# Tokens of the line memory in the order 4p + j, and two-block maxima banks masked on TensorE and reduced by VectorE

## The chip, the cores and the metric

One NeuronCore of a Trainium2 chip runs the whole kernel. The metric is the device time of one execution in microseconds (us), as a median of several runs. The profile shows the engines TensorE (PE, with its weight loads as PEld), VectorE (DVE), ScalarE (ACT), GpSimd (POOL) and the DMA queues that SyncE (SP) and the others start.

## The reference

The input is 8 batches of 512 tokens of width 256. Per batch an attention block runs, then a layer norm, then a mixture of experts (4 experts, the best 2 of each token) with a second layer norm. What the change touches is in the attention block:

```python
scores = einsum('bhtd,bhsd->bhts', q, k) * scale; causal mask; softmax; seq_out = attn @ v      # 16 heads of 16
write_lines, read_lines = exterior(w1, w2), exterior(r1, r2)        # 6 numbers per token and head, unit length
outer = Jw[..., :, None] * Jw[..., None, :]                         # 6 x 6 per token and head
M_all[t] = decay**t * sum over s < t of outer[s] * decay**(-s)      # a decayed prefix sum over the tokens
rd_M = einsum('bhti,bhtij->bhtj', rd, M_all); score_M = rd_M . rd; score_M2 = rd_M . rd_M
gated = mean over heads of sigmoid(mem_score * mem_scale) * gate
x = layernorm(x + (seq_out + gated * mem_val) @ out_w.T + out_b)
```

## The kernel before

Each engine has its own program and runs it in order. All follow one list of stages written out by hand, `stages_of_a_step` (L56); `run` (L468) walks it and calls, on each engine, the engine's own part of the stage. `schedule` (L481) makes nine steps, 0 to 8. In step i the batch i is in its first half (maxima of scores, queries and keys of batch i+1), the batch i-1 in its middle (scores, values, lines, memory, late maxima) and the batch i-2 at its end (o_tokens, z, projection, layer norm, routing). So one step holds parts of three batches, and steps 2 to 6 hold all of them. After step 8 come the 35 tiles of the experts (L1518 and L1531 on TensorE), which the change leaves alone.

**Maxima.** For a numerically safe softmax every query row needs the maximum of its masked scores. `maxima` on TensorE (L1350) makes a piece of 512 columns in one of three PSUM banks: per pair of heads five pieces, `maxima_blocks` (L539), with the widths 512, 512, 384+128, 384+128 and 256+256. A batch has 40 pieces, 20 in `maxima` (batch i) and 20 in `late_maxima` (batch i-1). On VectorE `maxima` (L1918) takes one custom instruction for each block of a piece: it adds the mask `mask_ts`, takes the maximum, and a second small instruction reads the accumulator out into a column of `maxes`. TensorE writes piece n only when VectorE has read piece n-3 (`sm_read`), and `maxima_to_rows` (L1378) turns the 20 maxima of a half when all are read.

**Line memory.** The token of partition p and block c is 128c + p. The lines of a batch (`lines_in`, `lines_out`, the six products at L888, L891) are normalised by `norms` (L1930) on VectorE, and GpSimd makes `outer` (L909) and two more blocks in which a decayed earlier block is added (L915, L918). TensorE's `memory` (L1384) makes the prefix sums over tokens: for each head one matmul with a decay matrix of 128 x 128 over 144 columns (4 blocks of 36), and one with the matrix of the block before over 108 columns. It goes in six parts of three heads (the last of one) through the two banks `ms_ps`. VectorE's `memory` (L1954) multiplies each part by the read lines (432 numbers) and sums over six. In the next step `memory_scores` (L1968) makes the two scores from `rdm`, `memory_gates` and `gates` the gate.

**The order around it.** Late in a step VectorE's `rank` (L1894) makes the places of the routed rows; GpSimd's `scatter` (L837) then issues eight indirect DMAs and loads the next residual. SyncE's store (L606) writes the layer-norm output in blocks of 128 tokens. ScalarE's `exps` (L1103) takes the exponential of each scores piece; TensorE writes piece n when piece n-2 is done.

## Time and profile before

| | us |
|---|---|
| median of 3 runs | 1076.8 (1074.87 to 1082.2) |
| profiled execution | 1076.55 |
| its span | 1074.9 |
| TensorE busy | 948.6 (88%) |
| VectorE busy | 738.0 (69%) |
| ScalarE busy | 603.7 (56%) |
| GpSimd busy | 444.0 (41%) |

The 1.65 us between the profiled execution and its span lie outside the first and last instruction. A busy time of TensorE counts overlapping matmuls once, but each matmul's own time is far longer than the distance to the next one, so work on TensorE is read from starts. Steps 0 to 8 end at about 626 us, the experts at about 1026 us; the last 49 us are the final layer norm and the stores.

### The profile page before, as it was taken

The numbers are of one execution on the slowest core, as the hardware profiler recorded it, in microseconds if no ns is written. First come the engines' busy times: TensorE is split into PE (matmuls) and PEld (weight loads), VectorE is DVE, ScalarE is ACT, GpSimd is POOL, SyncE is SP. The second block draws the span as 40 slices with busy tenths as digits, with TensorE's granted clock in tenths as the row PEclk, the third lists the DMA queues.
The fourth block names the chain that finished last, engine by engine and source line by source line (L and its number), as shares of the span: only waits on it lengthen the run. The fifth ranks groups of instructions, "written<-read, shape, count | busy, mean of one in ns | idle before, by whom it ended". The sixth has DMA issues, their size and how long they took to land. (4 is left out here: it accounts for less than half of the span.)

```text
span 1074.9 us, 26814 instructions
## 1 busy us (share of the span) xinstructions
PE 948.6 (88%) x8038; PEld 686.6 (64%) x8039; DVE 738.0 (69%) x2668; ACT 603.7 (56%) x1358; POOL 444.0 (41%) x398
## 2 busy tenths in 40 slices
PE   3698999897998997989979889999989989999970
PEld 1244656554655564565545668888879869889860
DVE  4637797795896996978868668876555655555663
ACT  3155554562563554545535668776676656666653
POOL 6437064273363543654544633322322433222243
PEclk8689999998999999999999999999999989999995
DMA  4785103213124033032030453232333323323264
GB/s 140 247 216 141 31 22 124 56 57 117 38 71 119 24 95 85 2 125 55 21 129 12 139 188 85 45 51 48 49 46 60 73 49 53 48 49 49 41 204 159
DMA packets 60852, 90.38 MB, mean 84 GB/s; under 512 B 8700, under 2 KB 50192, under 8 KB 59696
## 3 DMA queue, kind: packets, MB, share of 16 engines
q1 hardware_dynamic: 45336, 62.20, 20.4%
q0 software_dynamic: 14112, 22.42, 11.2%
q10 hardware_dynamic: 1280, 4.19, 1.0%
q8 instruction: 67, 1.10, 0.5%
q14 instruction: 57, 0.47, 0.1%
HBM read 52.79 MB, written 35.86 MB: 82 GB/s over the span
## 5 line engine op out<-in xcount | busy, mean ns | idle before, releaser
L1926 DVE CUSTOM_DVE_ANT_0 junk<-sm,mask_ts 128x512 bf16<-128x512 f32 (+3 forms) x512 | 220.4, 487 | 58.0 <-PE sm L1366 55.8
L1110 ACT ACTIVATE arena_b<-st 128x512 f32<-128x512 f32 x320 | 180.9, 599 | 136.7 <-PE st L1328 89.8
L950 POOL DMA_INDIRECT sums<-arena_b x66 | 109.9, 1666 | 273.9 <-DVE arena_b L2135 263.6
L2098 DVE TENSOR_TENSOR arena_b<-arena_b 128x256 f16<-128x256 f32 x280 | 116.4, 427 | 109.6 <-ACT arena_b L1185 99.4
L1326 PE MATMUL st<-arena_a 128*128 128x384 f16 (+3 forms) x512 | 129.4, 309 | 29.0 <-issue 19.0
L1366 PE MATMUL sm<-arena_a 128*128 128x512 f16 (+3 forms) x512 | 113.7, 311 | 12.1 <-DVE maxes L1926 6.2
L1518 PE MATMUL st<-arena_b,arena_a 128*128 128x256 f16 x840 | 116.2, 276 | 1.6 <-ACT arena_b L1185 1.6
L1518 PE MATMUL sm<-arena_b,arena_a 128*128 128x256 f16 x840 | 115.1, 273 | 2.3 <-issue 2.3
L1531 PE MATMUL pv<-arena_a,arena_b 128*128 x864 | 116.7, 273 | 0.0
L1531 PE MATMUL sm<-arena_a,arena_b 128*128 x816 | 112.9, 274 | 3.1 <-issue 3.1
L1326 PEld LDWEIGHTS st<-arena_a 128*128 128x128 f16 x512 | 50.9, 99 | 87.0 <-issue 45.2
L1346 PE MATMUL pv<-arena_b 128*32 128x512 f32 (+3 forms) x1024 | 97.9, 478 | 8.1 <-ACT arena_b L1110 6.4
L1181 ACT ACTIVATE arena_b<-sm,arena_b 128x256 f32<-128x256 f32 x140 | 67.0, 478 | 67.5 <-PE sm L1518 48.1
L1181 ACT ACTIVATE arena_b<-st,arena_b 128x256 f32<-128x256 f32 x140 | 66.8, 477 | 60.0 <-PE st L1518 40.9
L844 POOL DMA_INDIRECT slots<-res,slot_i x64 | 62.8, 981 | 90.1 <-DVE slot_i L1915 72.7
L1328 PE MATMUL st<-mask_st,ident_b 128*128 128x128 bf16 x512 | 97.5, 224 | 0.0
L1518 PEld LDWEIGHTS sm<-arena_b,arena_a 128*128 x840 | 82.2, 98 | 13.6 <-issue 3.7
L1518 PEld LDWEIGHTS st<-arena_b,arena_a 128*128 x840 | 82.5, 99 | 13.1 <-issue 3.0
L1531 PEld LDWEIGHTS pv<-arena_a,arena_b 128*128 128x128 f16 x864 | 84.5, 98 | 9.9
L1531 PEld LDWEIGHTS sm<-arena_a,arena_b 128*128 128x128 f16 x816 | 79.9, 98 | 13.5 <-issue 4.0
L1366 PEld LDWEIGHTS sm<-arena_a 128*128 128x128 f16 x512 | 41.9, 100 | 57.5 <-DVE maxes L1926 29.1
L1284 PE MATMUL ms<-arena_b 128*128 128x208 f16 (+2 forms) x576 | 70.8, 275 | 4.3 <-DVE zs L2008 4.1
(335 smaller groups left out, 1756.5 us busy)
## 6 DMA issues: line engine op xcount, KB each, us to landing
arena_b<-slots SPq DMA_DIRECT2D x35, 260.0 KB
arena_a<-w SPq DMA_DIRECT2D x8, 1024.0 KB, 6.2
arena_b<-x_tr SPq DMA_DIRECT2D x8, 512.0 KB, 4.1
q_rows<-arena_b SPq DMA_DIRECT2D x32, 128.0 KB
k_rows<-arena_b SPq DMA_DIRECT2D x32, 128.0 KB
arena_a<-q_rows SPq DMA_DIRECT2D x32, 128.0 KB
arena_a<-k_rows SPq DMA_DIRECT2D x32, 128.0 KB
res<-x_tok POOLq DMA_DIRECT2D x8, 512.0 KB, 6.4
```

What stands on the lines that cost most here:

```text
L950: pool.indirect_dma_start(sums, bass.IndirectOffsetOnAxis(ap=token_now[:, 1 - par, m:m + 1], axis=0), y_out[1 - par][:, m, :], None, compu ...
L1110: act.activation(probs[:, q, :], st_ps[piece % 2][:, :], ACT.Exp, scale=SCORE_SCALE).then_inc(exp_done, 1)
L1181: act.activation(g_32[:, hc % 4, :], u_bank(hc)[:, 0:ROWS], ACT.Gelu, bias=b1_now[:, par, hc:hc + 1], scale=1.0 / W_SCALE).then_inc(gelu_d ...
L1284: last = pe.matmul(out, xs[b_par][:, kc, shift:shift + P], ws[:, kc, cols:cols + n_cols], start=start and kc == 0 and n == 0, stop=kc == K ...
L1326: pe.matmul(out[:, at:at + width], ks[:, h % 2, h // 2, s * P:(s + 1) * P], qs[:, h // 2, s * P:T], start=m == 0, stop=False, skip_group_c ...
L1328: last = pe.matmul(out[:, at:at + P], ident_b[:, :], mask_st[:, :], start=False, stop=True, skip_group_check=True)
L1346: last = pe.matmul(out[32 * hl:32 * hl + 32, s * P:T], v_aug[:, s, 4 * g + hl, :], probs[:, slot, col:col + width], start=cls == 0, stop=c ...
L1366: last = pe.matmul(sm_ps[n % 3][:, at:at + width], qs[:, j, tile * P:(tile + 1) * P], ks[:, p, j, 0:width], start=m == 0, stop=True, skip_ ...
L1518: last = pe.matmul(u_bank(hc)[:, 0:ROWS], w_by_expert[:, up_expert, at:at + P], xs[par][:, kc, :], start=kc == 0 and n == 0, stop=kc == KC ...
L1531: last = pe.matmul(y_ps[1 - par][:, m * D:(m + 1) * D], gs[1 - par][:, hc, m * P:(m + 1) * P], w_by_expert[:, down_expert, at + lo * CHUNK ...
L1926: last = dve.tensor_tensor_reduce(junk[:, n % 3, at:at + width], sm_ps[n % 3][:, at:at + width], mask_ts[:, T - width:T], 1.0, NEG, ALU.ad ...
L2098: dve.tensor_tensor(g_lo[par][:, hc, :], g_32[:, hc % 4, :], g_hi[par][:, hc, :], ALU.subtract).then_inc(hid_done, 1)
```

## The change

Five things change together.

1. **Order of tokens.** Partition p now holds the tokens 4p, 4p+1, 4p+2, 4p+3. Matmuls that used 128 neighbouring columns as weights now use every fourth one (`n::C`): `lines_in`, the half of `values_in` that makes `mem_val`, and the transposes of `o_tokens`. Input, store and token numbers follow.
2. **Prefix sums.** GpSimd adds the four outer products of a partition (three additions instead of two multiplications and two additions), and TensorE needs one matmul of 36 columns for each head, in two parts of eight heads. What a token gets from the up to three earlier tokens of its own partition (six pairs) is computed on GpSimd as vectors, partly before it waits for the norms (`pair_gain`), partly after `outer_done` (`near_rows`, `near_done`), and added by VectorE in `memory_scores`.
3. **Maxima.** For the pieces with two blocks TensorE adds the mask by a matmul of 256 columns (24 per batch), and VectorE takes the whole bank with one plain maximum. The last piece of a half is followed by a small reduction and a copy.
4. **Tables.** Powers of the decays are half as many and one small table is made by GpSimd.
5. **The list of stages** is written anew in places; `rank` stands ahead of maxima 17, and the second part of `memory` behind values 8.

```diff
-        ("maxima", 17), ("rank", 0), ("first_expert", 0), ("maxima", 18), ("scores", 33), ("memory", 2), ("maxima", 19), ("values", 8),
-        ("scores", 34), ("scores", 35), ("memory", 3), ("memory", 4), ("scores", 36), ("scores", 37), ("maxima_rows", 0), ("memory", 5),
-        ("first_rows", 0), ("scores", 38), ("values", 9), ("scores", 39), ("values", 10), ("values", 11),
+        ("scores", 31), ("maxima", 16), ("tables", 0), ("scores", 32), ("values", 7), ("rank", 0), ("first_weights", 3),
+        ("first_expert", 0), ("maxima", 17), ("maxima", 18), ("scores", 33), ("maxima", 19), ("values", 8), ("memory", 1),
+        ("scores", 34), ("maxima_rows", 0), ("scores", 35), ("scores", 36), ("scores", 37), ("first_rows", 0), ("scores", 38),
+        ("values", 9), ("scores", 39), ("values", 10), ("values", 11),
...
+                    for own in range(C - 1):
+                        m, at = C - 1 - own, FIRST_PAIR[own]
+                        seen = chain(pool.tensor_tensor(pair_parts[:, at:at + m], read[:, own + 1:C, :, ::-1],
+                                                        write[:, own:own + 1].broadcast_to([P, m, H, NL]), ALU.mult))
...
                     pool.wait_ge(ninv_done, n_of(b + 1))
...
+                    for to, of in ((0, 1), (2, 3), (0, 2)):
+                        if (to, of) != (2, 3):
+                            pool.wait_ge(pool_chain, n_of(seen))
+                        last = pool.tensor_tensor(outer[:, to, :, :], outer[:, to, :, :], outer[:, of, :, :], ALU.add)
...
+                    last.then_inc(outer_done, 1)
...
+                    pool.tensor_tensor(near_rows[:, 3:C], near_rows[:, 3:C], pair_parts[:, 5:6], ALU.add).then_inc(near_done, 1)
...
                     if n == 0 and later(i, 2):
-                        act.wait_ge(sq_done, n_of(b))
+                        act.wait_ge(near_done, n_of(b))
...
-                    project(out[:, :], 1 - par, COL_VM, 512, 2 + n * P, True).then_inc(vm_ready, 1)
+                    project(out[:, 0:D], 1 - par, COL_VM, D, slice(2 + n * P, 2 + n * P + P), True)
+                    project(out[:, D:2 * D], 1 - par, COL_VM + D, D, slice(2 + n, 2 + T, C), False).then_inc(vm_ready, 1)
...
+                    if piece % 5 >= 2:
+                        blocks = sm_ps[n % 3][:, :].rearrange("p (n t) -> p n t", t=P)
+                        last = pe.matmul(blocks[:, 2:4] if piece % 5 < 4 else blocks[:, 1::2], mask_st[:, :], ident_b[:, :].unsqueeze(1).broadcast_to([P, 2, P]),
+                                         start=False, stop=True, skip_group_check=True)
...
+                        last = pe.matmul(out[:, hl * size:(hl + 1) * size], decay_t[:, heads * q + hl, :], outer[:, 0, heads * q + hl, :],
+                                         start=hl == 0, stop=hl == heads - 1, skip_group_check=True)
...
-                        last = pe.transpose(out[:, g * P:(g + 1) * P], o_t[:, g, n * P:(n + 1) * P], ident[:, :])
+                        last = pe.transpose(out[:, g * P:(g + 1) * P], o_t[:, g, n::C], ident[:, :])
...
+                    if kind < 2:
+                        col = 32 * kind + 4 * j + 3
+                        dve.tensor_tensor_reduce(junk[:, n % 3, :], bank[:, :], mask_ts[:, :], 1.0, NEG, ALU.add, ALU.max, maxes[:, col:col + 1]).then_inc(sm_read, 1)
+                    elif kind < 4:
+                        dve.tensor_reduce(of_blocks[:, kind - 2, at, :], bank[:, :].rearrange("p (n t) -> p n t", t=P), AX.X, ALU.max).then_inc(sm_read, 1)
...
+                            dve.tensor_reduce(of_half[:, :, :, 2], of_blocks[:, :, :, 0:3], AX.X, ALU.max)
+                            last = dve.tensor_copy(of_half[:, :, :, 0], of_blocks[:, :, :, 3])
...
+                    for n in range(C):
+                        rows = read_scaled[:, H * n + heads * q:H * n + heads * q + heads, ::-1]
+                        last = dve.tensor_tensor(mr[:, n], ms_ps[q][:, 0:heads * NL * NL].rearrange("p (h a e) -> p h a e", a=NL, e=NL),
+                                                 rows.unsqueeze(2).broadcast_to([P, heads, NL, NL]), ALU.mult)
...
+                    m_chain(dve.tensor_reduce(rdm[:, q].rearrange("p c h a -> p (c h a)"), mr.rearrange("p c h a e -> p (c h a) e"), AX.X, ALU.add))
...
+                    s_chain(dve.tensor_tensor(by_half(rdm[:, :, 1:C]), by_half(rdm[:, :, 1:C]), near_rows[:, 1:C].rearrange("p c (q h) e -> p q c (h e)", q=2), ALU.add))
```

## Rows read from the trace of the kernel before

**Rows 1.** Busy time by stretch: us, busy us (instructions) per engine, clock, DMA, GB/s
```profile
core 0: us, PE busy (x) PEld busy (x) DVE busy (x) ACT busy (x) POOL busy (x), PEclk, DMA share, GB/s
343.00:414.70 71.70, 65.88 (x554) 41.00 (x553) 57.62 (x220) 37.62 (x84) 36.06 (x31) 0.98 0.28 77
...
626.00:1026.00 400.00, 389.53 (x3500) 345.72 (x3499) 250.53 (x841) 273.25 (x627) 121.06 (x77) 0.99 0.32 57
```

**Rows 2.** The same view, step 5 cut into stretches
```profile
343.00:359.00 16.00, 15.78 (x139) 9.97 (x139) 14.85 (x48) 9.64 (x26) 5.77 (x3) 1.00 0.38 83
359.00:375.00 16.00, 14.76 (x109) 9.01 (x108) 14.04 (x59) 9.26 (x21) 10.95 (x11) 1.00 0.12 34
375.00:391.00 16.00, 15.88 (x136) 9.12 (x135) 14.91 (x62) 11.13 (x24) 10.71 (x9) 1.00 0.22 67
391.00:408.00 17.00, 14.10 (x137) 11.20 (x133) 13.02 (x52) 4.59 (x10) 5.84 (x6) 1.00 0.37 118
```

**Rows 3.** Timeline of TensorE: start us, us, instruction [idle before it and its releaser]
```profile
374.91 0.39 PE L1381 MATMUL sm<-ident,maxes 128*16 128x128 f32 x2 [0.71 <-DVE maxes L1926]
...
392.05 0.41 PE L1396 MATMUL ms<-outer,arena_a 128*128 128x144 f32 x2
...
392.51 0.43 PE L1396 MATMUL ms<-outer,arena_a 128*128 128x144 f32 x2
```

**Rows 4.** Timeline of VectorE, one round of five maxima pieces in step 0
```profile
44.63 0.69 DVE L1926 CUSTOM_DVE_ANT_0 junk<-sm,mask_ts 128x512 bf16<-128x512 f32 x1
...
45.24 0.69 DVE L1926 CUSTOM_DVE_ANT_0 junk<-sm,mask_ts 128x512 bf16<-128x512 f32 x1
...
47.92 0.69 DVE L1926 CUSTOM_DVE_ANT_0 junk<-sm,mask_ts 128x512 bf16<-128x512 f32 x1
```

**Rows 5.** Timeline of VectorE, a memory part and the instruction behind it, step 5
```profile
395.14 0.61 DVE L1961 TENSOR_TENSOR mr<-ms,lines 128x432 f32<-128x432 f32 x1 [0.25 <-PE ms L1398]
395.78 0.60 DVE L1964 TENSOR_REDUCE rdm<-mr 128x72 f32<-128x432 f32 x1
396.30 0.68 DVE L1926 CUSTOM_DVE_ANT_0 junk<-sm,mask_ts 128x512 bf16<-128x512 f32 x1
```

**Rows 6.** Groups of instructions by line and shape, VectorE: busy us, mean ns, idle before
```profile
L1964 DVE TENSOR_REDUCE rdm<-mr 128x72 f32<-128x432 f32 x40 | 24.1, 603 | 1.4
...
L1979 DVE TENSOR_TENSOR mr<-rdm,lines 128x384 f32<-128x384 f32 x8 | 4.9, 612 | 0.0
...
L1983 DVE TENSOR_TENSOR mr<-rdm 128x384 f32<-128x384 f32 x8 | 7.5, 932 | 0.3
```

**Rows 7.** Chain that ended last, in the experts, and 16 narrow matmuls on TensorE
```profile
792.54 0.66 PE st L1518 x6
...
316.98 1.90 PE L1441 MATMUL ms<-w_r,z_t 128*128 128x4 f32 x16
```

**Rows 8.** Groups of weight loads on TensorE, by shape
```profile
L1284 PEld LDWEIGHTS ms<-arena_b 128*128 128x128 f16 x576 | 39.8, 98 | 26.5 <-DVE zs L2008 6.5 <-issue 0.4
...
L1408 PEld LDWEIGHTS ms<-ident,o_t 128*128 128x128 f32 x128 | 14.9, 148 | 6.3 <-DVE zs L2008 3.9 <-issue 1.2 <-ACT o_t L1122 0.2
```

**Rows 9.** GpSimd in step 5 (timeline), and its narrowest line products by shape
```profile
378.27 0.86 POOL L900 TENSOR_TENSOR t<-lines,ninv 128x384 f32<-128x384 f32 x1 [4.55 <-DVE ninv L1942]
...
388.04 1.40 POOL L918 TENSOR_TENSOR outer<-outer 128x576 f32<-128x576 f32 x1
...
L888 POOL TENSOR_TENSOR t<-pts 128x128 f32<-128x128 f32 x16 | 10.4, 672 | 0.0
```

**Rows 10.** Timeline of all engines around the scatter of step 5
```profile
400.63 1.01 POOL L844 DMA_INDIRECT slots<-res,slot_i  x1 [11.18 <-DVE slot_i L1915]
...
407.86 0.60 ACT L1110 ACTIVATE arena_b<-st 128x512 f32<-128x512 f32 x1 [6.06 <-remote]
...
408.51 0.28 PE L1326 MATMUL st<-arena_a 128*128 128x256 f16 x1 [3.41 <-issue]
...
412.32 0.31 DVE L1961 TENSOR_TENSOR mr<-ms,lines 128x144 f32<-128x144 f32 x1 [4.56 <-remote]
```

More of the change, by code:

```diff
@@ L76, in stages_of_a_step @@
-        ("x1_rows", 3), ("first_weights", 2), ("scores", 27), ("maxima", 11), ("maxima", 12), ("maxima", 13), ("scores", 28),
-        ("gates", 0), ("logits", 0), ("values", 6), ("scores", 29), ("scores", 30), ("maxima", 14), ("memory", 0), ("memory", 1),
-        ("first_weights", 3), ("maxima", 15), ("scores", 31), ("maxima", 16), ("tables", 0), ("scores", 32), ("values", 7),
-        ("maxima", 17), ("rank", 0), ("first_expert", 0), ("maxima", 18), ("scores", 33), ("memory", 2), ("maxima", 19), ("values", 8),
@@ L798, in powers_of_decays @@
                 pool.wait_ge(decay_set, 2)
-                n, done, zero = 1, 0, 2 * P - 1
+                n, done, zero, power = 1, 0, P - 1, 5
                 while n < T - 1:
@@ new lines, in step @@
+                    last.then_inc(outer_done, 1)
+                    seen = chain(pool.tensor_tensor(write_unit.rearrange("p c h e -> p (c h) e"), lines[:, 0, 0:3 * H, :],
+                                                    ninv[:, 0, 0:3 * H].unsqueeze(2).broadcast_to([P, 3 * H, NL]), ALU.mult))
+                    pool.wait_ge(pool_chain, n_of(seen))
+                    for own in range(C - 1):
+                        m, at = C - 1 - own, FIRST_PAIR[own]
+                        to = near_rows[:, 1:C] if own == 0 else pair_parts[:, at:at + m]
+                        seen = chain(pool.tensor_tensor(to, pair_gain[:, at:at + m].unsqueeze(3).broadcast_to([P, m, H, NL]),
+                                                        write_unit[:, own:own + 1].broadcast_to([P, m, H, NL]), ALU.mult))
@@ L1391, in memory @@
                             pe.wait_ge(turned, 4)
-                    out = bank(q % 2, cs_read, 6 * b + q + 1)
-                    size = C * NL * NL
-                    for hl, h in enumerate(range(3 * q, min(3 * q + 3, H))):
-                        pe.matmul(out[:, hl * size:(hl + 1) * size], decay_t[:, h, 0:P], outer[:, h, 0:C, :].rearrange("p c e -> p (c e)"),
-                                  start=hl == 0, stop=False, skip_group_check=True)
-                        last = pe.matmul(out[:, hl * size:(hl + 1) * size - NL * NL], decay_t[:, h, P:2 * P],
-                                         outer[:, h, C - 1:C + 2, :].rearrange("p c e -> p (c e)"), start=False, stop=True, skip_group_check=True)
+                    out = bank(q, cs_read, 2 * b + q + 1)
+                    size, heads = NL * NL, H // 2
+                    for hl in range(heads):
+                        last = pe.matmul(out[:, hl * size:(hl + 1) * size], decay_t[:, heads * q + hl, :], outer[:, 0, heads * q + hl, :],
+                                         start=hl == 0, stop=hl == heads - 1, skip_group_check=True)
                     last.then_inc(cs_ready, 1)
@@ L2231, in lay_out @@
     return {
[L2232 removed]
+        "x_tok": x.reshape(B, P, C, D), "x_tr": x.reshape(B, T, KC, P).transpose(3, 0, 2, 1),
         "w_proj": by_part(w.T), "qk_bias": qkv_b[order].reshape(4, P).T,
```

246 lines of the change are left out of this document (145 added, 101 removed).

## Prediction

> **What bounds the kernel now.** I read the page first, then the busy time by stretch, then the timeline of one full step, then the groups by shape, last the waits. The experts take 400 us with TensorE nearly always busy [rows 1], and the change does not touch them; what it can move lies in the first 626 us, steps 0 to 8. Steps 2 to 6 last 71 to 77 us each, and I take step 5, 343.0 to 414.7 us, as their pattern: 71.7 us, TensorE busy 65.9, VectorE 57.6, GpSimd 36.1 [rows 1]. A share for the whole step misleads, so I cut it [rows 2]. From 343 to 375 (call it the early part: late maxima, o_tokens, lines, values, projection) VectorE is busy 28.9 of 32 us and TensorE idles at places, for VectorE's maxima among them (0.71 us before the maxima rows) [rows 3]. From 375 to 391 both are busy over 90%. From 391 VectorE is dense until about 404; then an odd end follows, read in the last part of the sum. So VectorE bounds the early part, both engines together bound the middle, and a saving of one alone is not paid out whole.
>
> **What each part costs.** First the maxima on VectorE. A round of five pieces takes 47.92 - 44.63 = 3.29 us from start to start where VectorE is never idle, a piece of 512 columns 0.61 [rows 4]. Afterwards two pieces stay as they are (2 x 0.61). The three others become one plain reduction of 512 numbers each. No row shows a reduction out of PSUM. The nearest is the one of 432 numbers in SBUF: 603 ns, and 396.30 - 395.78 = 0.52 us to the next start [rows 5, 6]. 80 numbers more at the pace between 384 and 512 would add under 0.1, so I take 0.60 us; as bounds I keep 0.52 (the row itself) and 0.69 (the custom instruction's own time [rows 4]). The round is then 2 x 0.61 + 3 x 0.60 = 3.02, 0.27 less; four rounds in a half save 1.1 us. The small reduction, its wait and the copy at the end of a half I take at 0.45 together (bounds 0 and 0.6, the latter one whole reduction of 432 numbers [rows 6]). Net -0.6 us per half, -1.2 per batch. As many numbers pass through VectorE as before (512 for 384 + 128): only the per-instruction part is saved.
>
> The memory on VectorE: a part of 432 costs 0.64 + 0.52 = 1.16 us [rows 5], five of them and a small one about 6.4 us a batch. After it there are per half four products of 288 and one sum of 1152. At the same pace (0.64 for 432, about 1.05 ns a number above a fixed 0.15) four products are about 1.6 and the sum 1.3, so 5.75 for both halves: -0.65 us. The same 2304 numbers pass again.
>
> Memory scores: one addition of 288 more and the product of 384 cut in two. Rows: 612 ns for a product of 384 with two inputs in SBUF, but 932 ns for the next one of the same size [rows 6]. I take +0.8 us (0.5 to 1.3). VectorE per batch: -1.2 - 0.65 + 0.8 = -1.05 us.
>
> TensorE. A head costs 392.51 - 392.05 = 0.46 us in memory [rows 3], 16 heads 7.4 us. Afterwards a head is two passes of 36 columns behind a full fp32 weight load. The nearest row is 16 passes of 4 columns with fp32 weights in 1.90 us, 0.12 each [rows 7]: 32 x 0.12 = 3.8. That saves 3.6 us a batch, all of it in the middle of the step. The masks add 24 matmuls of 256 columns, 0.66 / 6 = 0.11 us each [rows 7]: +2.6, 1.3 early and 1.3 in the middle. The weights taken with a step of four columns (lines, half of values, o_tokens) are not in the trace. Below, they cost nothing more. Above, I double the load of each: 98 ns for fp16 and 148 for fp32 [rows 8]. A pass that is shorter than its load then waits for it: for 48 matmuls of lines and 16 transposes that is up to 3.6 us a batch, all early. I take 0.9. TensorE per batch: -3.6 + 2.6 + 0.9 = -0.1, split into +2.2 early and -2.3 in the middle.
>
> A rule speaks against this. Row: contiguous fp32 weights of a transpose load in 148 ns, fp16 ones in 98 [rows 8]. The Trainium skill, page "SBUF — State Buffer", section "Door 1: The DMA port swizzle", says in a note that SBUF lines are 16 bytes and that accesses reach full rate only with two or more hits in a line. A step of four fp16 numbers would have two hits, one of four fp32 numbers one, so by it only the o_tokens would pay, at most 1.8 us of early TensorE time a batch instead of my 0.9; no row here shows a stepped load.
>
> GpSimd gets seven new instructions before it waits for the norms, in a wait of 4.55 us in step 5 [rows 9]. The two wide products are priced like others of their size. The narrow ones step through memory, like those of 128 numbers at 672 ns [rows 9]. Together about 3.9 us, so the wait covers them; with no cover they would delay `outer_done` by their own length, and a slack stands behind it: GpSimd is done at 388.04 + 1.40 = 389.4 [rows 9] and TensorE starts memory at 392.05 [rows 3], 2.6 us later. After the norms: one more product of 384 (0.86 [rows 9]), two multiplications of outer less, one addition more: equal within 0.3 us. About 3 us of near rows follow `outer_done`; the 11.18 us in which the scatter waits for VectorE's slots [rows 10] cover them, and so behind them in GpSimd's queue the eight scatters and the residual's load are not later. `near_done`, at about 392.5, holds ScalarE's lines_out and VectorE's memory scores of the next step, which begins at 414.7 [rows 1], 22 us later. Were it late, the exponentials would stand behind it on ScalarE and the late maxima on VectorE. The new tables on GpSimd stand in an idle stretch before step 1. Half as many powers, shorter turns and a larger SyncE store block are hidden as well: zero, 1 us at most.
>
> **The sum.** Step 0 has one half of maxima with VectorE as the bound: -0.6. Middle of a full step: VectorE gives -0.6 - 0.65 = -1.25 and TensorE -2.3; both are dense, so between them, nearer to the lesser: -1.6. Early part: VectorE +0.2, TensorE +2.2, part of which fills its idle places: +0.3. That is -1.3 a step. Eight steps (1 to 8; the last has no first half of maxima, but is TensorE's and ScalarE's, where -3.6 counts more) give -10.4. Total -11.0. Against the profiled execution: 1076.55 - 11.0 = 1065.55, and I say 1065.5. That execution lies 0.25 below the median of the runs, so the same holds there.
>
> The end of a step is what I can price least. While GpSimd issues the eight scatters (from 400.63 on), a ScalarE exponential starts 6.06 us late, TensorE idles 3.41 us, and the last memory product on VectorE comes 4.56 us late, though its inputs were there [rows 10]. The new list puts `rank`, and so the scatter, ahead of maxima 17 to 19 and memory 1. I count no change: behind rank VectorE needs 3 x 0.61 + 0.45 = 2.3 us for the three maxima, and its late start begins at 412.32 - 4.56 = 407.8, 7 us after the first scatter (ScalarE's at 401.8, 1.2 us after it).
>
> **Rivals.**
> *A. The whole of TensorE's saving is paid, and the end of the step shrinks.* TensorE is dense in the middle [rows 2]; if VectorE's waits for it hide inside its busy share, -2.3 a step counts, and an earlier scatter takes 1 us off the end of steps 2 to 7: 8 x -2.3 - 6 - 0.6 = -25, 1051.5. Against it: VectorE is dense in the same place.
> *B. The saving is swallowed early.* Masks and stepped weights put 2.2 us on TensorE where it has few idle places; if they cost 1 us more a step than I say, -11 + 8 = -3 is left: 1073.5.
> *C. Stepped weights load at half speed.* Early TensorE +4.9 instead of +2.2, of which idle places (1.5 us of 32 by the busy rows [rows 2], and what hides between) take nearly all of the first half: 8 x (+2.5) - 11 = +9, 1085.5. For it speaks the page above in part; against it that a load usually hides behind the matmul ahead of it.
> *D. The scatter meets the maxima.* If the late start of 4.56 us [rows 10] falls on maxima 17 to 19, TensorE stands at the maxima rows, which precede scores 35, and cannot pass: 6 steps x 4.5 - 11 = +16, 1092.5, slower. It decides when VectorE still has a maximum of the first half to take when its late starts begin, somewhere between 1.2 and 7 us after the first scatter.
>
> **How the numbers follow.** About 1% can be told from no change here, 10.8 us. Chances: the forecast 0.40 (1061 to 1070 is its own range), A 0.20, B 0.22, C 0.08, D 0.10. The forecast straddles the 1% line at 1066.0: of its 0.40 I count 0.23 as faster. With A that is 0.43. Same is 0.17 + 0.22 + most of C (0.05) = 0.44; slower is D and the rest of C, 0.13. The range leaves out the far end of A and of D: 1050 to 1084.
>
> **What would show it.** The reduction from PSUM at about 690 ns, next start after 0.60. Memory on TensorE at 3.8 us a batch. Stepped weight loads no longer than 98 and 148 ns, or else C. GpSimd's wait for the norms shrunk from 4.55 us to under 1, with no wait of TensorE for outer. Steps 2 to 6 about 1.3 us shorter each, and the experts at 400 us. I am wrong if a new wait stands before the maxima rows (D), or if a step changes by over 3 us without the middle having changed.

## The result, and the profile after

The kernel after takes 1094.8 us (1091.3 to 1100.3, 6 runs) where the kernel before takes 1080.0 on the same chip: a ratio of 1.0146, interval 1.0109 to 1.0182. It is slower, and outside the range. The later runs were on other chips, so each is compared with the kernel before on its own chip. On chip 11 (before 1078.8) the ratio of the same kernel was 1.0145 [1.0100, 1.0190]; on chip 9 (before 1054.1) it was 1.0015 [0.9993, 1.0037], no difference. (The first chip's number is not recorded.) So there are two things to explain: why 11 us of gain came out nowhere, and what costs 1.5% on chips like the first and nothing on chips like chip 9.

I cut every trace at the same three marks: the transfer to `o_t` of the last values, which ends a step; the late maxima rows on TensorE; and again the end. "Early" is from a step's end to the late maxima rows of the next step, "middle" from there to that step's end. Below are the early part of step 2 and both parts of step 5 (on chip 9 only the middle of step 5), first in the kernel before on the first chip (its step 5 whole is in [rows 1]). The expectations below call the early part of step 2, the first that is cut so, "the early part of step 1".

```profile
core 0: us, PE busy (x) PEld busy (x) DVE busy (x) ACT busy (x) POOL busy (x), PEclk, DMA share, GB/s
120.06:152.10 32.04, 30.72 (x245) 18.92 (x243) 28.32 (x106) 19.03 (x46) 13.26 (x11) 1.00 0.15 40
342.80:374.91 32.11, 30.66 (x244) 18.89 (x243) 28.80 (x106) 19.01 (x46) 16.72 (x13) 1.00 0.25 59
374.91:414.22 39.31, 35.16 (x310) 22.11 (x310) 28.63 (x114) 18.33 (x39) 19.34 (x18) 0.96 0.29 92
```

The kernel after, same chip:

```profile
113.87:146.88 33.01, 32.20 (x280) 23.31 (x279) 27.84 (x74) 18.95 (x46) 14.50 (x14) 1.00 0.14 39
340.60:377.88 37.28, 34.67 (x280) 24.71 (x279) 29.75 (x74) 19.27 (x46) 16.91 (x15) 0.92 0.19 46
377.88:418.06 40.18, 33.49 (x290) 19.21 (x291) 28.28 (x78) 18.81 (x38) 24.47 (x29) 0.91 0.29 92
```

The kernel before on chip 9:

```profile
119.21:151.24 32.03, 30.72 (x245) 18.91 (x243) 28.28 (x106) 18.97 (x46) 13.26 (x11) 1.00 0.13 40
363.71:397.15 33.44, 33.33 (x310) 21.81 (x310) 28.61 (x114) 18.15 (x38) 16.62 (x16) 1.00 0.31 95
```

The kernel after on chip 9:

```profile
117.73:150.73 33.00, 32.20 (x280) 23.32 (x279) 27.83 (x74) 18.95 (x46) 14.49 (x14) 1.00 0.14 39
364.85:398.00 33.15, 31.59 (x290) 18.90 (x291) 28.25 (x78) 18.65 (x39) 20.94 (x26) 1.00 0.29 92
```

Read the rows at full clock (PEclk 1.00) first. The early part of step 2 grew from 32.04 to 33.01 us on the first chip and from 32.03 to 33.00 on chip 9; it is 33.02 on chip 11. The middle on chip 9 went from 33.44 to 33.15: TensorE is busy 1.74 us less and the time is 0.29 less. VectorE's busy time fell by only 0.36. On the first chip the middle of step 5 is 6 to 7 us longer in either kernel, and that is not the change's doing.

Summed over the seven early parts (steps 2 to 8) and the middles of steps 1 to 7, from the profiled executions (us; "experts" is all that follows step 8, the final layer norm and stores too):

| | to late rows of step 1 | early | middle | step 8 | experts | span |
|---|---|---|---|---|---|---|
| before, first chip | 89.2 | 232.6 | 266.6 | 37.3 | 449.2 | 1074.9 |
| after, first chip | 84.2 | 250.9 | 264.0 | 37.4 | 456.2 | 1092.6 |
| before, chip 9 | 88.3 | 247.8 | 231.1 | 32.8 | 449.8 | 1049.8 |
| after, chip 9 | 85.9 | 247.9 | 233.4 | 33.1 | 456.4 | 1056.8 |
| after, chip 11 | 82.3 | 245.6 | 265.9 | 37.7 | 455.2 | 1086.7 |

The first column scatters between 80.7 and 89.2 over the runs of all kernels, so I read nothing from it. The loss on the first chip is 18.3 us early and 7.0 in the experts; the middles give 2.6 back and the first column 5.0. On chip 9 the profiled execution after is 7.0 us longer, and 6.6 of it lie in the experts.

The operations themselves, in the kernel after on chip 9, grouped by shape (count, busy us, mean ns, idle before them and its cause):

```profile
L1988 DVE TENSOR_REDUCE maxes_of_blocks<-sm 128x4 f32<-128x512 f32 x128 | 84.1, 685 | 25.8 <-PE sm L1420 25.5
L2032 DVE TENSOR_TENSOR outer_home<-ms,t 128x288 f32<-128x288 f32 x64 | 24.8, 450 | 4.8 <-PE ms L1452 4.8
L2036 DVE TENSOR_REDUCE rdm<-outer_home 128x192 f32<-128x1152 f32 x16 | 21.6, 1353 | 0.6
```

They are as forecast (about 690 ns the reduction, 1.3 us the sum). The prices of what VectorE was given were right; what happened to its other instructions was not foreseen.

In step 7 of the kernel after a new wait stands ahead of the maxima rows (first number the start, in brackets the idle time before it):

```profile
528.63 0.59 PE L1437 MATMUL sm<-ident,maxes 128*16 128x128 f32 x2 [2.74 <-DVE maxes L1997]
```

It is the same 2.74 us on the first chip and on chip 11. In this step alone `first_expert` gives VectorE 2.6 us of small instructions for the experts' order and tables (523.9 to 526.5), and the new list has it ahead of maxima 17 to 19 and the maxima rows ahead of scores 35 to 37. The middle of step 7 on chip 9 went from 33.28 to 35.92 us, at a clock of 1.00 and 0.90, while those of steps 2 to 6 became 0.2 to 0.3 shorter.

**GpSimd's "hidden" work stretches VectorE's.** Rows of the timeline of step 5 in the kernel after on chip 9 (start, length). VectorE's small instructions:

```profile
365.37 0.48 DVE L1902 TENSOR_TENSOR rs<-rs 128x4 f32<-128x4 f32 x1
366.97 0.43 DVE L2008 TENSOR_SCALAR n<-n 128x128 f32<-128x128 f32 x1
369.64 0.78 DVE L1910 SCALAR_TENSOR_TENSOR shift<-mean_var,rs 128x4 f32<-128x4 f32 x1
381.94 0.56 DVE L1931 TENSOR_TENSOR beaten<-lg 128x4 f32<-128x4 f32 x1
```

and GpSimd's at the same times:

```profile
365.16 0.67 POOL L918 TENSOR_TENSOR pts<-pts 128x288 f32<-128x288 f32 x1
366.89 0.43 POOL L923 TENSOR_TENSOR pts<-pts,pair_table 128x96 f32<-128x96 f32 x1
369.55 0.86 POOL L929 TENSOR_TENSOR t<-lines,own_power 128x384 f32<-128x384 f32 x1
381.83 0.64 POOL L958 TENSOR_TENSOR t<-t,pts 128x192 f32<-128x192 f32 x1
```

Add start and length: VectorE's end at 365.85, 367.40, 370.42 and 382.50, GpSimd's at 365.83, 367.32, 370.41 and 382.47. An instruction of VectorE on four numbers ends when GpSimd's wide one does. In the kernel before GpSimd stood in a wait of 4.55 us when the first two of these came, as in [rows 9], and between two instructions when the third did; they took (VectorE in step 5 on chip 9):

```profile
364.24 0.15 DVE L1844 TENSOR_TENSOR rs<-rs 128x4 f32<-128x4 f32 x1
365.51 0.23 DVE L1938 TENSOR_SCALAR n<-n 128x128 f32<-128x128 f32 x1
367.98 0.16 DVE L1852 SCALAR_TENSOR_TENSOR shift<-mean_var,rs 128x4 f32<-128x4 f32 x1
```

Over all eight batches on chip 9 the means went from 334 to 724 ns (`shift`), 151 to 362 (`rs`), 227 to 362 (the norms' maximum), and together from 632 to 1001 ns for the three comparisons of the logits: 1.1 us a batch. The Trainium skill, page "SBUF — State Buffer", section "Who interferes with whom", says that a VectorE instruction with two inputs in SBUF contends with a GpSimd instruction that reads SBUF, and that the later one waits for the whole of the other. The ends of `rs`, `shift` and `beaten`, 0.01 to 0.03 us after GpSimd's, agree; the norms' maximum (0.08 us after) has one input, so this sentence does not cover it. No run took GpSimd's new work away, so that this is what makes VectorE late in the middle is argued from these rows, not shown by an edit.

The kernel before has such meetings too, and on chip 9 they are larger than the change. VectorE's four gated sums into `zs` take 1.67 us together when alone; in step 8 of before_again (VectorE, GpSimd's residual and bias additions, TensorE):

```profile
545.44 5.87 DVE L2018 SCALAR_TENSOR_TENSOR zs<-arena_a,gated,zs 128x256 f32<-128x256 f32 x4
545.65 2.50 POOL L872 TENSOR_TENSOR res<-res,out_b 128x1024 f32<-128x1024 f32 x1 [8.59 <-DMA res<-x_tok]
548.12 2.52 POOL L875 TENSOR_TENSOR mv_odd<-mv_odd,mem_b 128x1024 f32<-128x1024 f32 x1
...
552.06 0.34 PE L1366 MATMUL sm<-arena_a 128*128 128x384 f16 x1 [2.90 <-DVE maxes L1926]
```

Single `zs` sums of 2.6 us instead of 0.48 stand there in steps 3, 5, 6, 7 and 8 of the kernel before and in steps 3, 5, 6 and 7 of the kernel after; on the first chip and chip 11 in none. So on chip 9 it matters where the additions fall: the early parts of steps 2, 3 and 4 grew by 1.0, 1.3 and 1.5 us, those of steps 7 and 8 shrank by 2.0 each, and the sum is equal. In it TensorE is busy 216.2 us before and 225.7 after; its idle time fell from 31.6 to 22.3.

**What the first chip adds.** Two things can be seen after the end of step 4: the residual's addition on GpSimd meets VectorE's near rows, and TensorE's lines then wait for VectorE's `zs` and run on at a lower clock. The timeline of the kernel after on the first chip, GpSimd's row, VectorE's and TensorE's:

```profile
344.81 2.36 POOL L887 TENSOR_TENSOR res<-res,out_b 128x1024 f32<-128x1024 f32 x1 [4.60 <-DMA res<-x_tok]
...
345.14 2.35 DVE L2054 TENSOR_TENSOR rdm<-rdm,t 128x288 f32<-128x288 f32 x1
...
351.99 4.57 PE L1333 MATMUL ms<-arena_b 128*128 128x64 f16 x36 [1.95 <-DVE zs L2088]
```

and the busy times of the stretch of the lines, of its part at half clock, and of the end of step 5, same kernel:

```profile
351.99:356.56 4.57, 4.57 (x38) 3.75 (x39) 4.13 (x11) 1.76 (x6) 0.00 (x0) 0.63 0.00 0
353.10:356.50 3.40, 3.40 (x24) 2.65 (x22) 2.96 (x10) 0.98 (x4) 0.00 (x0) 0.50 0.00 0
411.10:421.40 10.30, 7.17 (x42) 3.61 (x43) 2.24 (x7) 2.99 (x5) 3.46 (x4) 0.50 0.49 134
```

The addition of 288 numbers takes 2.35 us there and 2.38 in the next step; in the other steps, and on chip 9, where the two do not meet, it takes 449 ns. But the wait is not shown to come from the meeting: TensorE waits 2.25, 2.22 and 2.08 us for `zs` in steps 3, 7 and 8, where they do not meet. The granted clock was 1.00 before TensorE's wait and 0.63 over the lines that followed it: 3.4 us of that stretch at 1.2 GHz. In the kernel before the lines of step 5 had no such wait and ran at 1.00. Over the seven early parts the granted clock was 1.00, 0.96, 0.91, 1.00, 1.00, 1.00, 1.00 before and 1.00, 0.95, 0.88, 0.92, 0.95, 0.94, 0.95 after. If TensorE was busy throughout, the missing share of the clock times the length of each part is 4.8 us before and 15.0 after. These 10.2 us and 7 x 1.0 at full clock are 17.2 of the 18.3.

Most of the lost clock begins before the early part, in a step's last microseconds. Of the 29.5 us at 1.2 GHz in the seven early parts after, 22.7 are the ends of stretches that began in the step before, as at 411.10 above (the step ends at 418.06), where TensorE waits 1.38 and 2.44 us for ScalarE's exponentials, two of which start 2.3 us late; only 6.8 us, in steps 5 and 8, follow a wait for `zs`. In the kernel before such stretches reach 10.0 us into the early parts.

### The profile page after: what moved, and what is told of

The parts are those of the page before. It is cut to its first block and busy times, and to the rows that moved or that the text cites. A ratio compares the mean times of both kernels' runs of the same rounds, so it can differ in the third digit from the quotient of the medians.

```text
span 1092.6 us, 26611 instructions
## 1 busy us (share of the span) xinstructions
PE 950.1 (87%) x8170; PEld 702.9 (64%) x8171; DVE 735.4 (67%) x2127; ACT 604.5 (55%) x1357; POOL 507.2 (46%) x512
## 5 line engine op out<-in xcount | busy, mean ns | idle before, releaser
L1001 POOL DMA_INDIRECT sums<-arena_b x66 | 117.8, 1785 | 271.7 <-DVE arena_b L2215 261.3
L1986 DVE CUSTOM_DVE_ANT_0 junk<-sm,mask_ts 128x512 bf16<-128x512 f32 x128 | 84.9, 684 | 67.3 <-PE sm L1416 66.8
L1416 PE MATMUL sm<-arena_a 128*128 128x512 f16 (+3 forms) x512 | 116.3, 307 | 14.1 <-DVE maxes L1986 6.9
L1396 PE MATMUL pv<-arena_b 128*32 128x512 f32 (+3 forms) x1024 | 94.5, 467 | 18.3 <-ACT arena_b L1159 11.3
L1988 DVE TENSOR_REDUCE maxes_of_blocks<-sm 128x4 f32<-128x512 f32 x128 | 84.2, 685 | 25.7 <-PE sm L1420 25.5
L1585 PEld LDWEIGHTS sm<-arena_a,arena_b 128*128 128x128 f16 x816 | 80.5, 99 | 13.6 <-issue 3.6
L1333 PE MATMUL ms<-arena_b 128*128 128x256 f16 (+2 forms) x768 | 75.6, 256 | 10.6 <-DVE zs L2088 10.5
```

What stands on the lines that cost most here:

```text
L1001: pool.indirect_dma_start(sums, bass.IndirectOffsetOnAxis(ap=token_now[:, 1 - par, m:m + 1], axis=0), y_out[1 - par][:, m, :], None, compu ...
L1396: last = pe.matmul(out[32 * hl:32 * hl + 32, s * P:T], v_aug[:, s, 4 * g + hl, :], probs[:, slot, col:col + width], start=cls == 0, stop=c ...
L1416: last = pe.matmul(sm_ps[n % 3][:, at:at + width], qs[:, j, tile * P:(tile + 1) * P], ks[:, p, j, 0:width], start=m == 0, stop=True, skip_ ...
L1585: last = pe.matmul(y_ps[1 - par][:, m * D:(m + 1) * D], gs[1 - par][:, hc, m * P:(m + 1) * P], w_by_expert[:, down_expert, at + lo * CHUNK ...
L1986: dve.tensor_tensor_reduce(junk[:, n % 3, :], bank[:, :], mask_ts[:, :], 1.0, NEG, ALU.add, ALU.max, maxes[:, col:col + 1]).then_inc(sm_re ...
L1988: dve.tensor_reduce(of_blocks[:, kind - 2, at, :], bank[:, :].rearrange("p (n t) -> p n t", t=P), AX.X, ALU.max).then_inc(sm_read, 1)
```

## Experiments

Ratios are to the kernel before, run beside each kernel on its chip. Chip 1 (masks_only, no_masks, memory_behind_rank, contiguous_weights), 9 and 12 are like one another, with middles of 32 to 35 us in most full steps; chip 11 is like the first. The kernel after itself was not run on chips 1 and 12; the stretches of runs there are set against those of chip 9. (splits_off_the_adds, on chip 12, leaves these stretches as they are and has the same 33.00 and 33.15 us.)

**One part alone.** masks_only is the kernel before with the lines of the diff that touch `maxima`, on TensorE and VectorE; no_masks takes them out of the kernel after.

> The kernel before with one part of the change: the masks of the small maxima blocks on TensorE and plain reductions on VectorE; token order and order of the stages as before. Theory 1 (TensorE has no idle place in the early part of a step, 1.5 us of 32, so each matmul added there is paid): 12 masks of 0.11 us early = +1.3 us in each of steps 1 to 8, +10 in all, and about -0.3 a step in the middle from VectorE: about +8 us, 1088. Theory 2 (VectorE bounds the early part, as the prediction had it): -0.6 us a half, -8 to -9 in all: 1071.

> The kernel after without the masks on TensorE: maxima as in the kernel before, token order, memory and order of the stages as in the kernel after. Theory 1 (masks are paid on TensorE): about 8 us shorter than the kernel after, 1087. Theory 2 (VectorE bounds): 8 us longer than the kernel after, 1103. If the token order alone makes the loss, this is 1090 or more.

Masks alone 1.0039 [1.0012, 1.0067], the rest alone 1.0011 [0.9977, 1.0046]. By stretches at full clock: masks alone make the early part of step 2 32.33 (+0.3, not +1.3) and the middle 34.35 (+0.9); the token order, memory and list alone 32.78 (+0.75) and 33.45 to 33.60 (0 to +0.15). So the 3.6 us that TensorE saves in memory gave nothing by themselves, masks by themselves cost, and together the middle comes out at -0.3: TensorE's saving pays for TensorE's masks and little else. Both theories fell for the early part: the masks are neither paid in full there nor a gain. The token order and the work that comes with it carry three quarters of the early loss.

**Weights with a step of four.**

```diff
-                        last = pe.transpose(out[:, g * P:(g + 1) * P], o_t[:, g, n::C], ident[:, :])
+                        last = pe.transpose(out[:, g * P:(g + 1) * P], o_t[:, g, n * P:(n + 1) * P], ident[:, :])
```

and the slices `2 + n::C`, `1 + n::C` of `values_in` and `lines_in` likewise.

> The kernel after with contiguous weights in o_tokens, lines and the tokens' half of values, in place of those taken with a step of four columns; so tokens of another order are taken there and the output is wrong, with the same number of operations of the same shapes. Theory 1 (weight loads on a dense TensorE are paid): the 96 passes of lines and values fall from 9.8 to about 8.5 us a step and the 16 transposes from 2.5 to 2.1: -1.7 us a step, -14 in all, 1081. Theory 2 (the waits for zs on VectorE decide): at most -4, 1091.

0.9984 [0.9959, 1.0010]; the early part of step 2 is 32.92 instead of 33.00, the middle 33.16 as before. The o_tokens' loads themselves, by shape, stepped in the kernel after on chip 9:

```profile
L1462 PEld LDWEIGHTS ms<-ident,o_t 128*128 128x128 f32 x128 | 18.0, 210 | 7.1 <-DVE zs L2088 4.3 <-issue 1.1 <-ACT o_t L1171 0.7
```

and contiguous in this experiment:

```profile
L1462 PEld LDWEIGHTS ms<-ident,o_t 128*128 128x128 f32 x128 | 15.1, 151 | 7.0 <-DVE zs L2088 4.1 <-issue 1.4 <-ACT o_t L1171 0.7
```

210 against 151 ns, and 112 against 100 in the mean for the fp16 ones: the step costs the load, but hardly the time (0.1 us a step). My upper bound for the fp32 ones was twice their load; the trace shows 1.4 times.

**Which queue the middle hangs on.** one_product_of_four takes 2.3 us a step from VectorE, memory_twice gives 3.5 to TensorE:

```diff
-                    for n in range(C):
+                    for n in range(1 if later(i, 2) else C):
                         rows = read_scaled[:, H * n + heads * q:H * n + heads * q + heads, ::-1]
```

```diff
-                    for hl in range(heads):
+                    for hl in [*range(heads), *range(heads)]:
```

> The kernel after, which from step 2 on leaves out three of the four products in each half of memory (2 x 3 x 0.39 us of VectorE's queue, all in the middle of the step); the memory's result is wrong, TensorE's, ScalarE's and GpSimd's work is the same. Theory 1 (what TensorE saved in the middle has become waits for VectorE's queue, which is as long): the middle, 33.15 us from the late maxima rows to the step's end, becomes 1.5 to 2.3 us shorter, and the end of step 8 comes 10 us or more earlier. Rival (ScalarE's exponentials and the last values set the middle): under 0.5 us a step.

> The kernel after with TensorE's memory passes made twice (the second round overwrites the first): 32 more passes, 3.5 us a step, all in the middle; nothing else changes. Theory 1 (what TensorE saved there has become slack, 1.6 us of 33.15 by the busy rows and up to 3 in waits): the middle grows by 0.5 to 2 us, not by 3.5. Rival (TensorE still bounds the middle, and the saving was lost elsewhere): it grows by 3 to 3.5, end of step 8 25 us later.

one_product_of_four: 0.9935 [0.9895, 0.9975]; the middle is 32.38 instead of 33.15, so 0.8 of the 2.3 us are paid. memory_twice, on chip 11: 1.0322 [1.0270, 1.0374]; the middles of steps 2 to 5 are 41.6 to 43.2 instead of 39.9 to 40.0, +2.1 in the mean of the four, and step 8 is 3.6 longer. The only one of the four at full clock, step 2, gives +1.5; the others ran at 0.88, 0.88 and 0.96. The whole time rose by 23.2 us over after_third for 28 us of added passes. So on chip 11, with the lower clock, what is added to TensorE is paid for the larger part, and on chips 9 and 12 what is taken from either engine for the smaller: neither theory is the whole. I read it as two queues of one length, of which the shorter only waits for the other.

**The order of the stages.**

> The kernel after with one stage moved: the first half of memory (4 products and a sum, 2.9 us on VectorE) stands behind rank instead of three maxima pieces ahead of it. Theory A (the end of a step is pinned to its first scatter: 13.6 us behind it in steps 2 to 5 of both kernels): the scatter comes 2 to 2.9 us earlier and the end of steps 2 to 8 with it, 14 to 20 us in all, 1075 to 1081. Theory B (the last exponentials and values on TensorE and ScalarE set the end): within 3 us of the kernel after. Theory C (late starts on VectorE now meet the last maxima of the half, rival D of the prediction): a new wait ahead of the maxima rows and a longer step, 1100 or more.

> The kernel after with the first half of memory behind rank, as in memory_behind_rank. On a chip with late starts during the scatters (before at 1075 us or more): theory A (the end of a step is pinned to its first scatter) gives the scatter 2.1 us earlier and the step's end 1.5 to 2.1 us earlier in steps 2 to 8, 10 to 15 us below the kernel after there, ratio 1.000 to 1.005; rival (late starts now meet VectorE's last maxima or memory): 1.0145 or more. On a chip without them: 0.998 as in memory_behind_rank.

> The kernel before with its memory 0 and 1 (2.3 us on VectorE) behind rank. With late starts: theory A gives the scatter 1.5 to 2.3 us earlier and 10 to 15 us less, ratio 0.987 to 0.99; rival: no change or more, since the late starts meet more of VectorE's work. Without them TensorE is dense in the middle (33.3 of 33.4 us), and theory A gives no change, 0.998 to 1.002.

All three edits move only entries of the list: ("memory", 0), in the last ("memory", 0) and ("memory", 1), to just behind ("rank", 0). Results: 0.9979 [0.9951, 1.0008] on chip 1; 1.0118 [1.0091, 1.0144] and 1.0036 [1.0016, 1.0057] on chip 11. The first of the eight scatters of step 5 on chip 11, in the timeline of the kernel after:

```profile
403.15 1.01 POOL L859 DMA_INDIRECT slots<-res,slot_i  x1 [8.42 <-DVE slot_i L1973]
```

and with memory behind rank:

```profile
401.47 1.01 POOL L838 DMA_INDIRECT slots<-res,slot_i  x1 [6.29 <-DVE slot_i L1952]
```

Counted from the late maxima rows that is 26.5 and 24.4 us: the scatter did move by 2.1. The end did not follow: it lay 13.4 us behind the first scatter in steps 2 to 5 and now lies 16.9 to 17.7 behind, and the middle grew from 40.0 to 41.5 to 42.1. In the kernel before, that of step 5 grew from 39.3 (first chip) to 42.8. My theory A, suggested by an end at 13.5 to 14.1 us behind the scatter in steps 3 to 5 of both kernels, was a coincidence.

What the middle lost, the early part won back: with memory behind rank on chip 11 all seven early parts of the kernel after run at a clock of 1.00, 231.1 us in sum instead of 245.6, against middles of 279.1 instead of 265.9. The half-clock stretches now end before the step does. With the same place of memory in both kernels the early parts of steps 2, 3, 5 and 6 are 33.0 against 31.8 to 32.0 us: the added 1.0 us of a step, on this chip too. The two ratios, 1.0118 and 1.0036, lie 0.8% apart, where after_third alone is at 1.45%. On chip 11 and the first chip, what VectorE and ScalarE still have to do when the scatters start is what starts late. The list of waits calls the cause "remote": no instruction of this core is seen to release it (us in total, times, longest). In the kernel before on the first chip:

```profile
ACT arena_b L1110 <- remote: 43.7, 12, 8.2
DVE mr L1961 <- remote: 21.3, 5, 5.2
```

In the kernel after there:

```profile
ACT arena_b L1159 <- remote: 18.5, 6, 3.7
```

In the kernel before with memory behind rank, on chip 11:

```profile
DVE mr L1940 <- remote: 40.5, 6, 7.5
ACT arena_b L1089 <- remote: 33.5, 14, 5.2
```

More of VectorE's memory behind the scatters, more of it late: 40.5 us instead of 21.3. The lists of waits of chips 1, 9 and 12 have no such wait among their longest, and on chip 9 the end of step 5 lies 7.7 us (before) and 6.6 us (after) behind the first scatter. On chip 1 the edit makes the middle 0.9 longer too, and its 0.9979 is no gain that can be told.

> The kernel after with the first half of memory behind rank (as in memory_behind_rank) and the memory scores behind the last of the four o_tokens. Theory 1 (TensorE's wait of 2.0 to 2.4 us for zs, behind VectorE's memory scores, is paid in every step): 2 us less in each of steps 1 to 8 than memory_behind_rank, 14 to 16 us, ratio to before 0.983. Rival (VectorE is as late for the following maxima, and the wait moves there): no change, ratio 0.998.

> scores_behind_tokens without the masks on TensorE. Theory 1 (a matmul added to TensorE in the early part is paid, 1.3 us a step, and VectorE's 0.6 there not): 5 to 8 us less than scores_behind_tokens. Rival (with the waits gone VectorE bounds): 3 to 8 us more.

1.0012 [0.9978, 1.0045] and 1.0027 [1.0004, 1.0050]: taking the masks out as well makes no difference that can be told, so neither theory of reordered_no_masks came true. The waits of TensorE from the middle of step 1 to the end of step 8, in memory_behind_rank:

```profile
PE ms L1312 <- DVE zs L2067: 6.8, 4, 2.1
```

and in scores_behind_tokens:

```profile
PE ms L1312 <- ACT pts L1128: 6.6, 4, 2.0
```

The same lines wait as often and as long, now for ScalarE's `pts`: the rival was right, the wait moved, if to another engine than it said.

> The kernel after with the stages in the order of the kernel before (memory 0 and 1 in the places of its memory 1 and 3). Theory 1 (the loss is in the work, the order only moves waits): ratio to before 0.998 to 1.004, early part of step 1 33.0 or 0.2 less. Rival (the new order makes the loss, o_tokens 1 ahead of scores 1, z 0 early, rank ahead of maxima 17 to 19): early part of step 1 32.3, middle 32 or less, ratio 0.99.

On chip 11, 1.0089 [1.0054, 1.0124] with middles of 39.0 instead of 39.9 and the early part of step 2 at 33.05. The new order carries up to 0.6 of the 1.5%, in the middle; the early loss is the work's. The intervals of this and of after_third touch, so its size is not certain.

**The early part and the near rows.**

> The kernel after without the addition of the near rows on VectorE (0.45 us alone, 2.35 where it met GpSimd's residual addition), so the memory's result lacks them. Theory 1 (VectorE's memory scores stand ahead of the zs that TensorE waits for, 2.0 to 2.4 us in some steps): the early part of step 1, 33.0 us, becomes 32.5, and the other steps 0.5 to 1 less. Rival (TensorE's added passes make the early part): 33.0 stays.

> The kernel after with the masks on TensorE only for the first half of the heads, whose maxima lie in the middle of a step; the late maxima as in the kernel before. Theory 1 (in the early part TensorE is dense and pays 12 x 0.11 us, VectorE's 0.6 is not paid back): 1.0 to 1.3 us less from a step's end to the late maxima rows where the clock is full (33.0 before the edit in step 1), end of step 8 6 to 10 us earlier. Rival (VectorE bounds there): 0.6 us more a step.

near_add_left_out drops the first addition of `memory_scores`; masks_in_the_middle has `if piece % 5 >= 2 and not half_no` on TensorE and the old pieces on VectorE for the second half. On chip 11 the first gives 1.0082 [1.0058, 1.0107], and 32.76 early in step 2; the second, on chip 12, 1.0030 [0.9988, 1.0072] and 32.77. Each is worth 0.2 of the 1.0, the steps of the weights 0.1. About 0.4 of the early us stays without an owner. Against after_third the ratio fell from 1.0145 to 1.0082, more than 0.2 us a step would give, but the intervals touch. TensorE still waits 1.2 to 1.8 us for `zs` in five steps without the addition, so it is not what makes these waits.

**The experts.** The change touches none of their work, and still they took 7 us more in both pairs, all of it before tile 8 (from VectorE's first instruction of tile 0 to that of tile 8: 89.9 and 102.9 us on the first chip, 94.1 and 103.4 on chip 9; tile 0 starts before step 8 ends, so this stretch can grow by more than the 7 us). Some sums' adds were issued by GpSimd in 5.4 us, usually 1.55. splits_off_the_adds moves VectorE's weight splits from the first to the second half of tiles 1 to 5; splits_and_masks has both edits.

> The kernel after with the experts' weight splits (1024 numbers, two inputs in SBUF, 1.2 us each on VectorE) taken from the first half of tiles 1 to 5 into the second half, so that none follows the start of a scattered sum add. Theory 1 (an add's issue on GpSimd of 5.4 or 3.9 us, usual 1.55 to 1.75, is held up by VectorE's splits that run at the same time): no issue over 2.8 us is left, and the stretch from tile 0 to tile 8, 101 us in after_again, comes down to 90 to 94. Rival (the sums' traffic or the order of the tokens makes them long): they stay, and the stretch is 99 or more.

> Both edits of splits_off_the_adds and masks_in_the_middle together. Theory 1 of both: the two gains add, 14 to 18 us below the kernel after, ratio to before 0.985 to 0.99. Rival of either: that one's gain is missing.

GpSimd's sums in the kernel after on chip 9, and below them TensorE's wait for the slots in tiles 0 to 8:

```profile
L1001 POOL DMA_INDIRECT sums<-arena_b x66 | 117.7, 1783 | 266.3 <-DVE arena_b L2215 256.0 <-issue 10.4
...
PE ms L1311 <- DMA arena_b<-slots: 5.4, 3, 3.4
```

The same two with the splits moved, and a wait that is new:

```profile
L1001 POOL DMA_INDIRECT sums<-arena_b x66 | 107.8, 1633 | 275.0 <-DVE arena_b L2215 264.7 <-issue 10.4
...
PE ms L1311 <- DMA arena_b<-slots: 2.8, 3, 1.2
PE st L1572 <- DVE arena_a L1689: 4.4, 1, 4.4
```

The long issues are gone (the longest left is 2.4 us) and the waits for slots halved, so theory 1 is right on the adds; but TensorE now waits 4.4 us for one of the moved splits (L1689), and the stretch from tile 0 to tile 8 is 101.6 us instead of 103.4 (99.2 instead of 101.1 from tile 1 to 9, which is what the expectation counts), not 90 to 94. The ratios are 1.0021 [0.9978, 1.0064] and 1.0076 [1.0044, 1.0107]. Over all runs the stretch lies between 88.8 and 103.4. The new order of the tokens alone does not make it long: the four runs that have it together with memory 0 behind rank are at 88.8 to 94.7, with a step 8 that is 1.5 to 6 us longer. What makes it 94 in one kernel and 103 in another stays open, and so does why splits_and_masks has the highest ratio on chip 12.

**The same kernels again.**

> The kernel before, unchanged, for its trace on the chip of this call (on the chip of the first experiments the end of a step lay 6.6 to 8 us behind its first scatter, on the first chip 13.6). Ratio 1.00. If the chip makes the difference, its end of step lies 7 to 8 us behind the first scatter; if the edits made it, 13.6.

> The kernel after, unchanged, on the same chip. If the loss is TensorE's added work in the early part and the waits there (a cause that every chip has), the ratio is 1.01 or more again, with 3 to 5 us more from a step's end to the late maxima rows and 1.5 us less from there to the maxima rows. If the loss came from the late starts during the scatters, the ratio is 1.00 or less where these are absent.

> The kernel after, unchanged, on the chip of this call. If 1.0146 was that chip's and that pair of executions' own, the ratio is 0.998 to 1.004 again and the middle of a step 33.15 us; if the change costs this everywhere, 1.01 or more and the middle 40 us as on the first chip.

0.9996 [0.9959, 1.0033], 1.0015 [0.9993, 1.0037] and 1.0145 [1.0100, 1.0190], read above. The chip makes the late starts: end behind first scatter 7.7 us in before_again, 13.6 in the kernel before on the first chip. On chip 9 the early parts are equal in sum, 247.8 and 247.9 us, though TensorE has 1.0 us more to do in each: it fills idle time that the `zs` sums which meet GpSimd, shown above, leave in either kernel. That is read from the rows and not shown by an edit. (The early part of step 4 is long in either for another reason, a wait for the rows of the next batch: 4.2 us for `q_rows` before, 3.6 for `k_rows` after.) That a ratio near 1.0145 comes with the late starts is seen on the first chip and chip 11; what in them makes the change dearer beyond the clock was not tried. No kernel that computes all of the reference beat the kernel before by more than its interval.

## Why the prediction was wrong, point by point

- **The operations.** Reduction from PSUM, memory's products and sum and its passes on TensorE (3.85 us for 3.8): right within 5%. The stepped fp32 loads lie between my two bounds. (The 3.6 and 1.8 us for them cannot be worked out from [rows 8], where 48 x 98 + 16 x 148 ns are 7.1 us; at 0.1 us measured nothing hangs on them.) The near rows' addition takes 449 ns where it meets no GpSimd instruction, up to 2.38 us where it does. TensorE's busy time in the middle fell by 1.74 us, I had 2.3.
- **The middle, "-1.6, between them, nearer to the lesser": wrong, -0.3 at full clock.** Two terms failed. VectorE's saving of 1.25 us shrank to 0.36 of busy time, because I costed GpSimd's new work at nothing: I asked whether it fits into GpSimd's own wait (3.9 us in 4.55 [rows 9]; it did in step 5, where TensorE did not wait for `outer`, but in step 1 on chips 9 and 11 TensorE waited 1.2 us for it) and not whom it disturbs while it runs. By the rows it costs VectorE 1.1 us a batch. And a saving between two dense engines is not the mean of both: one_product_of_four was paid for a third, and TensorE's 1.74 us with VectorE's 0.36 gave 0.29.
- **The early part, "+0.3": wrong, +1.0 at full clock.** This is the step that turns the sum: with +1.0 and -0.3 a step is 0.7 longer, not 1.3 shorter. I put 2.2 us of TensorE's work into its idle places. It was busy 30.7 of 32.0 us, and 1.5 us more work became 1.0 more time. The reading "VectorE bounds the early part" [rows 2, 3] was half the truth: TensorE's waits were 1.3 us of 32.
- **Step 0, the start, the end.** Step 0's 0.6 cannot be told from a start that scatters by 8 us. "The end of a step: no change" held on time behind the scatter (13.6 and 13.6 in step 5), but the scatter came 0.8 later, not earlier: rank moved up in the list, memory 0 and logits did not get out of its way. That the half clock which follows the late starts reaches into the next early part was no term of the sum; it is most of what the first chip adds.
- **The experts at 400 us: wrong.** 7 us more in the profiled executions; cause open.
- **The rivals.** D gave 1092.5, nearly the time, by another mechanism: no late start met the maxima (in step 5 they were taken by 405.5, 1.1 us after the first scatter; the wait ahead of the maxima rows is 0.30). That D's number is near is luck. Its sign, a new wait before the maxima rows, is there in step 7 alone, 2.74 us, and no late start stands before it. B and C put the loss where most of it was, in the early part, but by passes and loads; what enlarged it on the first chip was TensorE's clock after the waits at a step's end and for `zs`. No rival had the clock in it, though the half clock after a step's end could be read in the trace before.
- **The range** left out 1094.8. It took the spread of each term, but not a slower clock after waits, nor that the effect differs between chips: 1.0145 and 1.0015.

## To carry to other kernels

Before work is called hidden on an idle engine, list the instructions of the other engines that run in that wait and read from the same memory: here 3.9 us that in most steps nobody waited for ran beside VectorE's smallest instructions while these took 1.1 us more. Between two engines that are both over 90% busy, a saving was paid here for a sixth to a third, and an addition to one for about half or more. Judge a change of 1% on more than one chip, and compare stretches at full clock before whole times.

## What the runs showed of the hardware that I had not expected

- VectorE's instruction on 128x4 numbers took 0.78 us instead of 0.16 beside a GpSimd product, and ended 0.01 us after it; one on 128x256 took 2.6 instead of 0.48 beside a GpSimd addition of 1024. A sum's add issued by GpSimd took 5.4 us instead of 1.55 while VectorE's splits ran, and no longer than 2.4 with these moved.
- Chips differ: on chip 11 and the first, ScalarE and VectorE start up to 8.2 us late while eight scatters are issued, and a middle of the kernel before takes 39.3 us there, 33.4 on chip 9.
- A transpose's fp32 weight load with a step of 16 bytes takes 210 ns, a contiguous one 151; the time of the kernel does not show it.
- After waits of TensorE at a step's end the granted clock was 0.50 for 10.3 us (411.10 to 421.40), 3.3 of them in the next step.
